# Softmax normalisation of the probability rows moved from VectorE to ScalarE in an attention and mixture-of-experts layer

## Chip, cores and metric

The kernel runs on all 8 cores of one Trainium2 chip, as one program on different data. The metric is device time in microseconds (us) of the slowest core. Two executions of the kernel before give 5368.27 and 5384.47 us, median 5376.37 us.

## The reference

Input `x` is (4, 2048, 2048) in float32. It is normalised per row (`_layernorm`, no affine part), and the layer returns `x + attention(xn) + moe(xn)`.

```python
q = heads(x @ Wq + bq); k = heads(x @ Wk + bk); v = heads(x @ Wv + bv)   # 16 heads of 128
scores = einsum('bhqd,bhkd->bhqk', q, k) / sqrt(2048)
scores = where(causal, scores, -inf)
attn = softmax(scores, axis=-1)
out = einsum('bhqk,bhkd->bhqd', attn, v) ... @ Wp + bp
# moe: 2 shared and 16 routed experts, 2048 -> 1408 -> 2048, relu;
# sigmoid router, the best 4 gates normalised; all experts are computed densely
```

## The kernel before

Each core takes half of one sequence: 1024 query rows of its own, 8 tiles of 128, against 2048 keys (its own 1024 and the sibling half's 1024, the latter masked by a bias `msk8`). The program has three stages.

- **p0** (lines 306 to 492): layer norm of the 16 row tiles, transposed by DMA into `xnf_own` and `xnf_sib`, and the router.
- **p1** (lines 522 to 889): attention, a loop over 16 heads `h`. Heads go in pairs: an even head first projects V for both (`wvb`, L810, 256 matmuls); an odd head ends with the output projection of both (L867, added into `acc` by VectorE at L884).
- **p2** (lines 898 to 1013): 18 experts, dense matmuls (L947, L954, L989).

Every engine has one queue in program order, written by the calls `T` (TensorE), `A` (ScalarE), `V` (VectorE), `DMA`; `wait=[...]` lists the tokens that an instruction waits for. An engine does nothing of what is queued behind a waiting instruction. The same Python order fills all queues.

For a query tile `tc` (0 to 7) of a head the pieces are:

- `plan_scores(tc)`: two matmuls of 512 keys of the sibling half (L664) into PSUM `psF[0]` and `psF[1]`, taken out by ScalarE (L674) into `scob`; then one or two matmuls for the own keys (L685) into the same two PSUM buffers, so that the first L685 waits until the first L674 has emptied `psF[0]`. The last own piece is taken out by VectorE (L695), another before it by ScalarE (L699). Then VectorE adds the diagonal mask (L705) and takes the row maximum (L711).
- `plan_scores_b(tc)`: ScalarE's exponential of the whole row, `L = (tc+9)*128` wide, float32 to bf16, with the row sum (L727); VectorE's reciprocal of the sum (L734) and the multiplication of the row by it (L737, bf16 in place in `prob`).
- `plan_transposes(tc)`: one DMA of SyncE's queue that transposes the row tile of `prob` into `atT` (L748). It waits for the normalised row and, since there is one `atT`, for the matmuls of the tile before that read it. `atT` lies on the same bytes as `wvb`.
- `plan_av(tc)`: `tc+9` matmuls of `atT` with V (L770) and ScalarE's evacuation into `outg` (L778).

`make_prep(h+1)` gives seven pieces for the next head: the weight DMAs, four K tiles (L564, 16 matmuls of 512 columns each, into `psF[4]` and `psF[5]`) and two Q tiles (L606, likewise). A head runs `plan_scores(0)`, `plan_scores(1)`, `plan_scores_b(0)`, `plan_scores(2)`, in even heads the V projection, and then for each `tc`:

```python
if tc + 1 < OWN: plan_scores_b(tc + 1)
if tc + 3 < OWN: plan_scores(tc + 3)
if nxt: nxt.pop(0)()          # one piece of the next head
plan_transposes(tc)
plan_av(tc)
```

So iteration 0 issues the weight DMAs, iterations 1 to 4 hold a K tile each, 5 and 6 a Q tile; iterations 0 to 4 hold scores of tile `tc+3`. Head 15 has no next head.

Of the kernel before, what the change touches and what calls it, by code (L numbers as in the profile page):

```python
# [11 lines left out]
AF = mybir.ActivationFunctionType  # L12
AX = mybir.AxisListType.X
ALU = AluOpType
# [136 lines left out]
def build_nc(dbg=False, phases=("p0", "p1", "p2")):  # L151
# [32 lines left out]
    def alloc(name, shape, dtype, off=None):  # L184
        if off is None:
            off = cur[0]
            per = int(np.prod(shape[1:])) * mybir.dt.size(dtype)
            cur[0] = (off + per + 31) & ~31
        return nc.alloc_sbuf_tensor_at(name, shape, dtype, offset=off)
# [19 lines left out]
    amx = alloc("amx", [128, 3, 8], F32)  # L209
# [26 lines left out]
    prob = alloc("prob", [128, 2, 2048], BF16, off=OVL + 60416)  # L236
# [15 lines left out]
    def B_(name):  # L252
        if name not in bufs:
            bufs[name] = Buf()
        return bufs[name]
# [4 lines left out]
    def V(fn, wait=()):  # L260
        return pl.on("vector", fn, wait, inc="ve")

    def A(fn, wait=()):
        return pl.on("scalar", fn, wait, inc="ac")
# [41 lines left out]
    if "p0" in phases:  # L306
        for ct in list(range(OWN, LCH)) + list(range(OWN)):
# [17 lines left out]
            for t_ in ts:  # L325
# [13 lines left out]
                                                 scale=-0.5), wait=[t1])  # L339
# [7 lines left out]
            if own:  # L347
# [11 lines left out]
                    scale=stab[:, ct, 0:1], bias=stab[:, ct, 1:2]),  # L359
# [6 lines left out]
                    scale=vt[:, sb, 2:3], bias=stab[:, ct, 1:2]),  # L366
# [22 lines left out]
            else:  # L389
# [7 lines left out]
                    scale=vt[:, sb, 2:3], bias=vt[:, sb, 3:4]),  # L397
# [124 lines left out]
    if "p1" in phases:  # L522
# [110 lines left out]
        for h in range(H):  # L633
# [84 lines left out]
            def plan_scores_b(tc, h=h):  # L718
                sl = tc % 3
                L = (tc + 9) * 128  # L720
                sc = B_("scob%d" % sl)
                am = B_("amx%d" % sl)
                pr = B_("prob%d" % (tc % 2))
                prold = pr.w()
                pr.wrd = {}
                pr.rdd = {}
                tex = A(lambda a, L=L, sl=sl, pp=tc % 2: a.activation(  # L727
                    prob[:, pp, 0:L], scob[:, sl, 0:L], AF.Exp, bias=amx[:, sl, 0:1],
                    scale=1.0, accum_out=amx[:, sl, 2:3]),
                    wait=[smx_tok[tc]] + prold)  # L730
                pr.did_w(tex)
                sc.did_r(tex)
                am.did_w(tex)
                trc = V(lambda v, sl=sl: v.reciprocal(amx[:, sl, 3:4], amx[:, sl, 2:3]),  # L734
                        wait=[tex])
                am.did_w(trc)
                tnm = V(lambda v, L=L, sl=sl, pp=tc % 2: v.tensor_scalar(  # L737
                    prob[:, pp, 0:L], prob[:, pp, 0:L], amx[:, sl, 3:4], None, ALU.mult),
                    wait=[trc, tex])
                pr.did_w(tnm)  # L740
                am.did_r(tnm)
                tnm_tok[tc] = tnm
# [46 lines left out]
            plan_scores(0)  # L789
            plan_scores(1)  # L790
            plan_scores_b(0)
            plan_scores(2)

# [38 lines left out]
            for tc in range(OWN):  # L832
                if tc + 1 < OWN:
                    plan_scores_b(tc + 1)
                if tc + 3 < OWN:
                    plan_scores(tc + 3)
                if nxt:
                    nxt.pop(0)()
                plan_transposes(tc)
                plan_av(tc)  # L840
# [252 lines left out]
```

How the kernel before makes its waits and increments, by code:

```python
            def _f(eng):  # L1027
                for ws, fn, inc, n in ops:
                    for s, v in ws:
                        eng.wait_ge(semh[s], v)
                    if fn is not None:
                        instr = fn(eng)
                        if inc is not None:
                            instr.then_inc(semh[inc], n)
```

## Time and profile before

| | |
|---|---|
| median of two executions | 5376.37 us |
| the profiled execution: device time | 4777.82 us |
| its span, slowest core (5) | 4776.3 us |
| spans of the 8 cores | 4756.1 to 4776.3 us |
| granted TensorE clock, mean of a core | 0.928 to 0.930 |
| stage p0, up to | 309 us |
| stage p1 | 309 to 1916 us, about 198.5 us for each pair of heads |
| stage p2 | 1916 us to the end |

The profile is of one execution, on core 5. Busy times of an engine are sums over its instructions. "Idle before, releaser" is time in which an engine did nothing before an instruction, and the instruction whose end it awaited. The chain of waits is followed back from the last instruction; a row of it is start, duration, and what was going on. "Clock" is the share of full speed granted to TensorE: 1.0 is 2.4 GHz, 0.5 is 1.2 GHz.

### The profile page before, as it was taken

What the parts mean: (1) busy time and instruction counts of PE and PEld (TensorE: products, weight loads), DVE (VectorE), ACT (ScalarE), POOL (GpSimd) and SP (SyncE); (2) the same over time, 40 slices, a digit from 0 to 9 for tenths busy, and PEclk for the clock granted to TensorE, in tenths of its full rate; (3) what the DMA queues carried; (4) which work ended last, traced back from release to release, by engine and by line L of the source; (5) the groups of instructions that cost most, each with busy time, mean ns of one, the idle gap of its engine ahead of it and who ended that gap; (6) DMA issues with size and microseconds to landing.
All of it is one profiled execution on the core that took longest, in us unless ns stands there. A gap on an engine that the chain in (4) does not pass through costs nothing.

```text
span 4776.3 us, 51141 instructions; the slowest of 8 cores (4756.1 to 4776.3 us)
## 1 busy us (share of the span) xinstructions
PE 3897.2 (82%) x19288; PEld 1852.9 (39%) x19288; DVE 1192.4 (25%) x1819; ACT 858.7 (18%) x1317; POOL 145.3 (3%) x256
## 2 busy tenths in 40 slices
PE   0036767667676675899999999999999999999997
PEld 0013424234243342344444444444444444444443
DVE  2223434434344344211112111221112111221112
ACT  2323232332323323001100011001100011001100
POOL 0000000000000000000000000000000000000000
PEclk9998878788787886699999999999999999999999
DMA  7332242322333223144434434344434434344434
GB/s 140 75 62 49 51 65 47 62 49 51 65 53 56 49 51 56 37 80 78 75 69 80 89 68 82 63 80 78 75 69 80 88 68 83 63 80 78 75 69 123
DMA packets 332254, 335.22 MB, mean 70 GB/s; under 512 B 300625, under 2 KB 301009, under 8 KB 307153
## 3 DMA queue, kind: packets, MB, share of 16 engines
q0 software_dynamic: 70848, 257.97, 29.6%
q1 hardware_dynamic: 260020, 65.60, 7.6%
q10 hardware_dynamic: 1152, 8.39, 0.4%
q8 instruction: 165, 2.70, 0.2%
q14 instruction: 69, 0.57, 0.0%
HBM read 499.69 MB, written 8.39 MB: 106 GB/s over the span
## 4 chain that ended last, share of the span: by engine, by line
PE 76%; DMA 10%; DVE 5%; issue 4%; ACT 4%; SPq 1%; DVEq 0%; ACTq 0%; POOLq 0%
PE psF L989 29%; PE psF L947 14%; PE psF L954 14%; PE psF L564 6%; DMA atT<-prob 6%; PE psF L810 5%; DVE acc L884 3%; PE psF L770 3%; ACT scob L674 2%; PE psF L908 1%; PE psF L867 1%; DMA atT<-wstream 1%; PE psF L606 1%; PE psF L685 1%; DMA lofm<-lobf 1%
## 5 line engine op out<-in xcount | busy, mean ns | idle before, releaser
L989 PE MATMUL psF<-w2b,hbuf 128*128 128x512 bf16 x6336 | 1370.4, 379 | 25.3 <-ACT hbuf L968 25.3
L947 PE MATMUL psF<-xnf_own,w1b 128*128 128x512 bf16 x3168 | 1201.8, 379 | 0.0
L954 PE MATMUL psF<-xnf_own,w1b 128*128 128x512 bf16 x3168 | 1201.7, 379 | 0.0
L989 PEld LDWEIGHTS psF<-w2b,hbuf 128*128 128x128 bf16 x6336 | 618.7, 98 | 777.0 <-issue 33.6
L1006 DVE SCALAR_TENSOR_TENSOR acc<-psF,gat,acc 128x512 f32<-128x512 f32 x512 | 384.2, 750 | 2071.9 <-PE psF L989 2071.9
L968 ACT ACTIVATE hbuf<-psF,b1t 128x512 bf16<-128x512 f32 x396 | 250.6, 684 | 2542.9 <-PE psF L947 2339.6
L947 PEld LDWEIGHTS psF<-xnf_own,w1b 128*128 128x128 bf16 x3168 | 310.2, 98 | 375.8 <-issue 2.8
L954 PEld LDWEIGHTS psF<-xnf_own,w1b 128*128 128x128 bf16 x3168 | 310.2, 98 | 374.3 <-issue 1.1
L770 PE MATMUL psF<-atT,vbuf 128*128 128x128 bf16 x1600 | 133.7, 245 | 179.8 <-DMA atT<-prob 177.9
L711 DVE TENSOR_REDUCE amx<-scob 128x1 f32<-128x1152 f32 (+7 forms) x128 | 232.9, 1819 | 13.3 <-DVE scob L705 0.2
L685 PE MATMUL psF<-kbuf,qbuf 128*128 128x512 bf16 (+1 forms) x192 | 73.5, 384 | 194.6 <-ACT scob L674 194.6
L884 DVE TENSOR_TENSOR acc<-acc,psF 128x512 f32<-128x512 f32 x256 | 175.9, 687 | 164.0 <-PE psF L867 137.3
L727 ACT ACTIVATE prob<-scob,amx 128x1152 bf16<-128x1152 f32 (+7 forms) x128 | 207.5, 1621 | 0.7 <-DVE amx L734 0.2
L674 ACT ACTIVATE scob<-psF,msk 128x512 f32<-128x512 f32 x256 | 161.3, 682 | 249.0 <-PE psF L664 247.3
L770 PEld LDWEIGHTS psF<-atT,vbuf 128*128 128x128 bf16 x1600 | 115.7, 110 | 217.5 <-issue 203.1
L431 PE MATMUL psF<-chl,xnf_own 128*128 128x16 bf16 x128 | 7.8, 174 | 226.2 <-DMA xnf_own<-xnbf 226.2
L867 PE MATMUL psF<-kbuf,outg 128*128 128x512 bf16 x256 | 94.9, 432 | 82.7 <-DMA atT<-wstream 47.4
L564 PE MATMUL psF<-xnf_own,wrA 128*128 128x512 bf16 x512 | 161.2, 486 | 0.0
L564 PE MATMUL psF<-xnf_sib,wrA 128*128 128x512 bf16 x512 | 144.7, 447 | 8.5 <-DMA wrA<-wstream 8.5
L664 PE MATMUL psF<-kbuf,qbuf 128*128 128x512 bf16 x256 | 102.2, 486 | 54.3 <-DVE scob L695 52.5
L685 PEld LDWEIGHTS psF<-kbuf,qbuf 128*128 128x128 bf16 x192 | 19.0, 99 | 294.1 <-issue 294.1
L810 PE MATMUL psF<-wvb,xnf_own 128*128 128x256 bf16 x1024 | 125.1, 289 | 0.3 <-DMA wvb<-wstream 0.2
(78 smaller groups left out, 1706.2 us busy)
## 6 DMA issues: line engine op xcount, KB each, us to landing
w2b<-wstream POOLq DMA_DIRECT2D x72, 1408.0 KB, 13.7
w1b<-wstream POOLq DMA_DIRECT2D x90, 1024.0 KB, 8.3
xstage<-xin POOLq DMA_DIRECT2D x16, 1024.0 KB, 7.0
w1b<-wstream POOLq DMA_DIRECT2D x18, 512.0 KB, 7.5
wrA<-wstream POOLq DMA_DIRECT2D x16, 512.0 KB, 6.5
wrB<-wstream POOLq DMA_DIRECT2D x16, 512.0 KB, 8.8
wvb<-wstream POOLq DMA_DIRECT2D x8, 1024.0 KB, 8.8
y<-acc ACTq DMA_DIRECT2D x8, 1024.0 KB, 11.8
```

Of the source, the lines that this page charges most:

```text
L564: mm = T(lambda t_, dc=dc, xt=xt, xo=xo, ps=ps: t_.matmul(ps[:], wrA[:, dc, :], xt[:, dc, xo:xo + 512], start=(dc == 0), stop=(dc == NCH - ...
L674: te = A(lambda a, j=j, sl=sl, ps=ps: a.activation(scob[:, sl, j * 512:(j + 1) * 512], ps[:], AF.Identity, scale=SCALE, bias=msk8[:, 0:1]) ...
L711: tmx = V(lambda v, L=L, sl=sl: v.reduce_max(amx[:, sl, 0:1], scob[:, sl, 0:L], axis=AX, negate=True), wait=sc.w() + amold)
L727: tex = A(lambda a, L=L, sl=sl, pp=tc % 2: a.activation(prob[:, pp, 0:L], scob[:, sl, 0:L], AF.Exp, bias=amx[:, sl, 0:1], scale=1.0, accum ...
L770: out_ps=out_ps, n=len(order): t_.matmul(out_ps[:, 0:128], vbuf[:, lci, hp * 128:(hp + 1) * 128], atT[:, slot, 0:128], start=(oi == 0), st ...
L810: mm = T(lambda t_, dc=dc, xt=xt, xo=xo, ps=ps: t_.matmul(ps[:, 0:256], xt[:, dc, xo:xo + 128], wvb[:, dc, :], start=(dc == 0), stop=(dc = ...
L884: tev = V(lambda v, tcq=tcq, dt=dt, ps=ps: v.tensor_tensor(acc[:, tcq, dt * 512:(dt + 1) * 512], acc[:, tcq, dt * 512:(dt + 1) * 512], ps[ ...
L947: mm0 = T(lambda t_, dc=dc, fci=fci, wslot=wslot, ps=ps0: t_.matmul(ps[:], w1b[:, wslot, dc, fci * 128:(fci + 1) * 128], xnf_own[:, dc, 0: ...
L954: mm1 = T(lambda t_, dc=dc, fci=fci, wslot=wslot, ps=ps1: t_.matmul(ps[:], w1b[:, wslot, dc, fci * 128:(fci + 1) * 128], xnf_own[:, dc, 51 ...
L968: te = A(lambda a, Fg=Fg, tt=tt, e=e, ps=ps: a.activation(hbuf[:, Fg, tt * 512:(tt + 1) * 512], ps[:], AF.Relu, bias=b1t[:, e, Fg:Fg + 1]) ...
L989: mm = T(lambda t_, fc=fc, tcq=tcq, wslot=wslot, ps=ps: t_.matmul(ps[:], hbuf[:, fc, tcq * 128:(tcq + 1) * 128], w2b[:, wslot, fc, :], sta ...
L1006: v.scalar_tensor_tensor(acc[:, tcq, dt * 512:(dt + 1) * 512], ps[:], gat[:, tcq, e - 2:e - 1], acc[:, tcq, dt * 512:(dt + 1) * 512], ALU. ...
```

## The change

The multiplication of the row by the reciprocal of its sum is issued on ScalarE as an activation `Identity` with the reciprocal as its per-partition scale, in place of VectorE's `tensor_scalar`. Its place in the Python order is the same, right behind the exponential and the reciprocal, so in ScalarE's queue it stands between the exponential of tile `tc+1` and the evacuations of the scores of tile `tc+3`. Its tokens are ScalarE's now; the transposing DMA and the next writers of `prob` wait for those.

```diff
                 trc = V(lambda v, sl=sl: v.reciprocal(amx[:, sl, 3:4], amx[:, sl, 2:3]),
                         wait=[tex])
                 am.did_w(trc)
-                tnm = V(lambda v, L=L, sl=sl, pp=tc % 2: v.tensor_scalar(
-                    prob[:, pp, 0:L], prob[:, pp, 0:L], amx[:, sl, 3:4], None, ALU.mult),
+                tnm = A(lambda a, L=L, sl=sl, pp=tc % 2: a.activation(
+                    prob[:, pp, 0:L], prob[:, pp, 0:L], AF.Identity,
+                    scale=amx[:, sl, 3:4]),
                     wait=[trc, tex])
                 pr.did_w(tnm)
                 am.did_r(tnm)
```

## Rows read from the trace of the kernel before

**Rows 1.** The page, busy time, share of the span and instructions of each engine.

```profile
PE 3897.2 (82%) x19288; PEld 1852.9 (39%) x19288; DVE 1192.4 (25%) x1819; ACT 858.7 (18%) x1317; POOL 145.3 (3%) x256
```

**Rows 2.** Windows: stretch, length, busy PE, PEld, DVE, ACT, POOL, clock, DMA.

```profile
748.00:947.00 199.00, 135.15 (x768) 71.94 (x768) 82.05 (x125) 64.13 (x105) 3.71 (x7) 0.83 0.32 55
1916.00:4776.00 2860.00, 2794.74 (x12736) 1259.79 (x12736) 450.23 (x608) 250.58 (x396) 106.82 (x180) 0.98 0.41 76
```

**Rows 3.** What L685 on TensorE waited for, all 192 (us, times).

```profile
  ACT scob L674: 194.6, 173
```

**Rows 4.** Timeline, iteration 2 of an even head: start, us, engine, line, operation.

```profile
793.63 1.27 ACT L674 ACTIVATE scob<-psF,msk 128x512 f32<-128x512 f32 x2
793.84 0.16 DVE L734 RECIPROCAL amx<-amx 128x1 f32<-128x1 f32 x1 [5.22 <-ACT prob L727]
794.11 0.62 DVE L737 TENSOR_SCALAR prob<-prob,amx 128x1536 bf16<-128x1536 bf16 x1
794.46 0.38 PE L685 MATMUL psF<-kbuf,qbuf 128*128 128x512 bf16 x1 [2.38 <-ACT scob L674]
```

**Rows 5.** Groups by shape: line, engine, shapes, count, busy us, mean ns, idle.

```profile
L727 ACT ACTIVATE prob<-scob,amx 128x2048 bf16<-128x2048 f32 x16 | 31.9, 1992 | 0.0
L727 ACT ACTIVATE prob<-scob,amx 128x1280 bf16<-128x1280 f32 x16 | 21.7, 1357 | 0.4 <-DVE amx L734 0.2
L727 ACT ACTIVATE prob<-scob,amx 128x1152 bf16<-128x1152 f32 x16 | 20.1, 1254 | 0.3
L395 ACT ACTIVATE xnbf<-xstage,vt 128x2048 bf16<-128x2048 f32 x8 | 16.7, 2093 | 6.0 <-DVE vt L391 3.5 <-DMA xnf_sib<-xnbf 2.5
L727 ACT ACT_TABLE_LOAD x1 | 1.3, 1283 | 0.1
L737 DVE TENSOR_SCALAR prob<-prob,amx 128x2048 bf16<-128x2048 bf16 x16 | 12.1, 753 | 1.7
```

**Rows 6.** Chain of waits, behind the V projection of an even head: start, us, what.

```profile
778.23 3.22 DMA atT<-prob
```

**Rows 7.** Timeline, iteration 6 of an even head.

```profile
830.73 0.75 DVE L737 TENSOR_SCALAR prob<-prob,amx 128x2048 bf16<-128x2048 bf16 x1
832.93 1.00 PE L770 MATMUL psF<-atT,vbuf 128*128 128x128 bf16 x15 [0.32 <-PE psF L606]
```

**Rows 8.** Timeline, start of an even head, ahead of its V projection.

```profile
747.24 1.27 ACT L674 ACTIVATE scob<-psF,msk 128x512 f32<-128x512 f32 x2
748.32 0.15 DVE L734 RECIPROCAL amx<-amx 128x1 f32<-128x1 f32 x1
```

**Rows 9.** Timeline of PE, ACT and DVE, start of an odd head.

```profile
849.94 0.48 PE L685 MATMUL psF<-kbuf,qbuf 128*128 128x384 bf16 x1 [0.50 <-ACT scob L674]
854.49 1.12 PE L770 MATMUL psF<-atT,vbuf 128*128 128x128 bf16 x9 [0.70 <-DMA atT<-prob]
...
852.37 1.27 ACT L674 ACTIVATE scob<-psF,msk 128x512 f32<-128x512 f32 x2 [0.49 <-PE psF L664]
...
850.88 0.55 DVE L695 TENSOR_SCALAR scob<-psF 128x384 f32<-128x384 f32 x1
853.47 0.15 DVE L734 RECIPROCAL amx<-amx 128x1 f32<-128x1 f32 x1
```

**Rows 10.** Timeline of PE in head 15, iterations 0, 2 and 4.

```profile
1838.00 1.12 PE L770 MATMUL psF<-atT,vbuf 128*128 128x128 bf16 x9 [1.51 <-DMA atT<-prob]
1848.41 1.33 PE L770 MATMUL psF<-atT,vbuf 128*128 128x128 bf16 x11 [0.79 <-DMA atT<-prob]
1860.03 1.55 PE L770 MATMUL psF<-atT,vbuf 128*128 128x128 bf16 x13 [0.81 <-DMA atT<-prob]
```

**Rows 11.** Chain of waits, K tiles of even and odd heads: start, us, what.

```profile
795.31 5.14 PE psF L564 x16
804.82 3.47 PE psF L564 x16
859.08 6.18 PE psF L564 x16
```

## Prediction

> **What bounds the kernel now.** I read the page first. ScalarE is busy for 858.7 us and VectorE for 1192.4 us of 4776.3 us [rows 1], so by busy time there seems to be room for an operation on either. That number decides nothing, so I went to the windows. The stage of the experts, from 1916 us on, keeps TensorE busy for 2794.7 of 2860 us [rows 2]; the change issues nothing there. A pair of heads takes about 199 us, and in it TensorE is busy for only 135 us, ScalarE for 64 and VectorE for 82 [rows 2]. No engine fills the stage: it is bound by a loop of waits, and the question is which engines' work lies in it.
>
> The third view answers that, what L685 waits for: 194.6 us in 173 waits, all for L674 [rows 3]. The chain of waits shows the loop in every iteration that has a K tile: L770 of one tile, L778, the exponential L727 of the next, the two L674, L685, the K tile's 16 matmuls L564, L770 again. The reason is the order of the queues. TensorE has put L664 into both PSUM buffers and can't issue L685, nor anything behind it (K tile, L770), before ScalarE has emptied the first; and ScalarE first has to do the exponential that stands ahead of L674 in its queue. The timeline shows what is not in the loop: VectorE's multiplication at 794.11 runs beside L674, which started at 793.63 [rows 4]. VectorE waited 5.22 us for the exponential before that. So VectorE has slack where ScalarE has none.
>
> **The change, part by part.**
>
> *Removed from VectorE*: 128 multiplications, 0.62 us at 1536 columns and 0.753 at 2048 [rows 4, 5], so by extrapolation 0.52 and 0.55 at the narrowest two, 1152 and 1280. They run beside ScalarE's evacuations, the cover that makes them nearly free. Only at a head's start do they stand ahead of VectorE's L695 of the next scores. I credit nothing for that, since ScalarE is later there after the change. The reciprocal stays.
>
> *Added to ScalarE*: 128 activations with a per-partition scale, in place in bf16. No row has this form. The nearest are the exponentials of the same widths with one per-partition operand: 1.254 us at 1152 columns, 1.357 at 1280, 1.992 at 2048 [rows 5], some 0.106 us for each 128 columns. An `Identity` to bf16 with two such operands took 2.093 at 2048 columns [rows 5]. So kind and function hardly matter, width does. The bounds are 0.753 us at 2048 columns, if ScalarE had VectorE's rate, and 2.093; I take the exponential's value, which is nearest in engine, operands and width.
>
> Here the skill speaks against the change: by the Trainium skill, ScalarE: Activation LUTs, Rules for kernel authors, a multiplication belongs on VectorE, which the page puts at up to about three times as fast for bf16 with one source. The rows say 1.992 against 0.753, or 2.6 times [rows 5]. By the page's three times the longest one would cost 2.26 us instead of 1.99, which is an estimate from the page and the row; the sum goes by the row.
>
> *The wait*: the new instruction waits on ScalarE for the reciprocal. Behind it in the queue stand the L674 of tile `tc+3`, for which L685 waits. In [rows 4] L674 starts at 793.63, the reciprocal at 793.84 with 0.16 us, and the multiplication that waits for it at 794.11. With the multiplication on ScalarE from 794.11 for 1.57 us (1536 columns, two steps above 1.357), and 0.09 us by which two ScalarE instructions overlap (two L674 of 0.68 us take 1.27), L674 starts at 795.59. That is its duration plus 0.39 us.
>
> *Iterations 1 to 4* of a head, each with the loop above: widths 1408, 1536, 1664 and 1792. By steps of 0.106 from 1.357 they take 1.46, 1.57, 1.68 and 1.78, in sum 6.49 us; with 4 x 0.39 that makes 8.05 us per head, all on the chain. Nothing takes it up again: the transposes are long landed when L770 starts.
>
> *Iterations 0 (even heads), 5, 6 and 7*: no cost. In iteration 0 of an even head the transpose behind the V projection takes 3.22 us [rows 6], and the scores of tile 3 would still end before it lands, about 0.4 us ahead by my count. In 5 and 6 there are no scores. The tightest is iteration 6: ScalarE's multiplication would run from 830.73 to 832.72, while the transpose that needs it waits for L770, which starts at 832.93 and ends at about 834 [rows 7]. What hides it is a Q tile and the single `atT`; without that cover it would cost some 1.2 us.
>
> *Start of an even head*: the reciprocal of tile 0 stands on VectorE behind the maximum of tile 1 and starts at 748.32, 1.08 us after the L674 of tile 2 [rows 8]. After the change L674 waits for it: 748.32 + 0.26 + 1.25 - 0.09 = 749.74, instead of 747.24. That is 2.50 us, which the L685 behind it passes on to the V projection.
>
> *Start of an odd head*: the same 2.50 us for tile 2. Then it cascades. L685 of tile 2 moves from 849.94 to 852.44 and its L695 to 852.96. From L695 to the next reciprocal VectorE has 2.59 us of work (850.88 to 853.47), so that comes at 855.55. The multiplication (1280 columns, 1.36) ends at 857.17 and L674 of tile 3 starts at 857.08 instead of 852.37: 4.7 us. L770 of tile 0 had waited 0.70 us for its transpose [rows 9], which takes up that much, and 4.0 us stay.
>
> *Head 15* has no K tiles and waits more for transposes. Its start costs 4.7 - 1.5 = 3.2 us, and iterations 1 to 4 cost 1.85, 1.96 - 0.79, 2.06 and 2.17 - 0.81 [rows 10], together 9.6 us.
>
> *TensorE's clock*: a K tile took 3.47 us where it was granted 1.0 all through, 5.14 where its first part ran at 0.5 (1.2 GHz) and 6.18 at an odd head's start, behind a stretch of sparse work [rows 11]. TensorE was idle for 2.38 us before L685 [rows 4], about as long in the other iterations, and behind most of these gaps the clock was at 0.5. On the chain an even head has one tile of 3.5 us and an odd head two. With 2 us more of idle time I expect that all of them begin at 1.2 GHz and cost at least 5.14: 8 x 1.67 + 7 x 2 x 1.67 = 37 us. The bounds are 0, and 92 us if every tile takes 6.18: 8 x (3 x 1.04 + 2.71) + 7 x (2 x 2.71 + 1.04). The Trainium skill has this direction too (TensorE: Matmul & The Clock Gate, Part 1: throttled is the default and activity releases it).
>
> *Sum*: 8 x (2.50 + 8.05) + 7 x (4.0 + 8.05) + 9.6 = 84.4 + 84.4 + 9.6 = 178 us, and with the clock 215 us. Against the profiled execution's own 4777.8 us that makes 4993 us. The two executions behind the median lie 599 us above it, and no view shows where; all added time is waiting in p1, so I carry the 215 us over unchanged: 5376 + 215 = 5591, or 4.0% more.
>
> **The rivals.**
>
> 1. *No clock term.* If the K tiles keep their mix of 3.5 and 5.1 us, the time is 5376 + 178 = 5554. For it: an idle stretch of 2.4 us already brings the fall in some iterations and not in others, so where the tiles fall may matter more than 2 us.
> 2. *A colder clock.* With every K tile at 6.18 us it is 5376 + 178 + 92 = 5646. For it: TensorE's idle time in a pair of heads would rise from 64 of 199 us to some 87 of 222. Against: once TensorE is busy, the clock has come back within the tile.
> 3. *A cheap multiplication.* Should ScalarE do it at VectorE's 0.5 to 0.7 us, an iteration costs 1.0 us rather than 2.0 and the total is near 90 us: 5466, within 2%. Against: no ScalarE row of that width is under 1.2 us.
> 4. *Off the chain* (the other side). If ScalarE's extra work ran under TensorE's, the removed VectorE work would be a small gain: 0.52 + 0.55 us ahead of L695 at each of 16 head starts, 17 us, so 5359, within 2%. This holds if L685 doesn't wait for L674; for it speaks ScalarE's 32% in the stage [rows 2], against it the 194.6 us [rows 3]. It decides only where L685 is ready at least 1.85 us after the first L674 has ended, and the wait says it is ready before.
> 5. *Freed weight loads.* The Trainium skill, SBUF — State Buffer, on who interferes with whom, has VectorE's fast modes lock GpSimd out while it writes descriptors for its DMAs. By rows: of the loads of GpSimd's queue only those of `wvb` and `wp` are on the chain, and 8 starts of 0.52 us would be 4 us of gain, too little to change the sign. It would make 5587 of my forecast.
> 6. *A table load with each `Identity`.* One load takes 1.28 us, and 256 would cost 328 us more. Against: there is one load at L727 in all [rows 5], though exponentials and `Identity` alternate throughout.
>
> **How the numbers follow.** My forecast, 178 us with a clock term of some 20 to 60 us, has a chance of 0.6 and gives 5574 to 5614. No clock term (or less than 178) has 0.18, the colder clock 0.12, the cheap multiplication 0.05, off the chain 0.03, freed loads 0.01 and table loads 0.01. The range 5515 to 5665 takes in the first three with the spread of the two executions shown (16 us) and an error of a fifth in the 178; it leaves out about 0.15. Two per cent, about what a measurement of this kernel tells from no change, is 107 us. Only rivals 3 and 4 end below that, so slower has 0.91, the same 0.08, and 0.01 is left for faster, of which I have no case.
>
> **What the changed profile would show.** The new ScalarE group should hold 128 instructions and about 207 us, with ScalarE near 1066 us and VectorE near 1111. L685's wait for L674 should rise from 194.6 us to about 400 (64 x 2 in the iterations, and the starts). The starts of an even head's V projection and of its first K tile should be 2.5 and 4.3 us later in the head; a pair of heads should take 22 to 27 us more, and p2 the same 2860 us. I am wrong if L674 starts right behind the exponential, if the new instructions are much shorter than 1.2 us, or if the K tiles' 3.47 us remain.

## The result and the profile after

The changed kernel is slower: the ratio to the kernel before is 1.0447, 95% interval 1.0403 to 1.0491. The median over all executions is 5163.38 us (13 of them, from 4992.57), and of the kernel before 4959.79 us (10, from 4770.66). In many executions of either kernel the cores of one die or both run at a lower granted clock (down to 0.79, where 0.93 before and 0.91 after are usual) and take longer; the ratio leaves those out, and the spans and stages below are of cores without it, on which the kernel before takes about 4775 us and the changed one 4993 to 5006.

The profiled executions have spans of 4776.3 us before (core 5) and 5004.0 us after (core 6), 227.7 us more. The added time is all in the stage of attention. From the first K tile's matmul to the first matmul behind the stage the 8 cores take 1612.3 us before and 1838.0 us after in the median, 225.7 us more; what follows takes 2843 to 2847 us in both.

The page of the changed kernel, busy time of each engine ([rows 1]). ScalarE has 202 us more, VectorE 80 us less. 335 of TensorE's 19288 matmul records are missing on this core, among them 127 in each of two lines of the experts' stage and 10 of the K tiles.

```profile
PE 3921.8 (78%) x18953; PEld 1868.4 (37%) x19288; DVE 1112.0 (22%) x1691; ACT 1060.7 (21%) x1445; POOL 145.9 (3%) x256
```

Windows of the changed kernel, a pair of heads and the stage of the experts, columns as in [rows 2]. The pair takes 228.7 us instead of 199, and TensorE is busy for only 5 us more in it; a window of the same length in the experts' stage looks as before.

```profile
761.20:989.90 228.70, 140.01 (x758) 73.76 (x768) 72.04 (x108) 89.42 (x120) 3.72 (x7) 0.79 0.27 48
2142.40:5002.40 2860.00, 2781.45 (x12482) 1260.27 (x12736) 450.23 (x608) 250.70 (x396) 107.32 (x180) 0.98 0.42 76
```

What L685 waited for in the changed kernel ([rows 3]: 194.6 us), on the profiled core 6, where 185 of 192 matmuls have a record. Core 1 has a record of each: 389.2 us after and 193.1 before. So the few waits of core 6 that are put down to "remote" seem to belong to the same stall.

```profile
  ACT scob L674: 365.4, 133
  remote: 29.4, 6
```

The new ScalarE groups by shape, narrowest and widest (columns as in [rows 5]). They are as long as the exponentials of the same width. The idle time ahead of them is the wait for the reciprocal: 20.4 us over 16 instructions for tile 0 and 19.5 for tile 1, some 1.2 us each, and 0.4 us each for the later tiles.

```profile
L737 ACT ACTIVATE prob<-prob,amx 128x2048 bf16<-128x2048 bf16 x16 | 32.0, 2002 | 6.9 <-DVE amx L734 6.9
L737 ACT ACTIVATE prob<-prob,amx 128x1152 bf16<-128x1152 bf16 x16 | 20.1, 1255 | 20.4 <-DVE amx L734 20.4
```

The timeline of the changed kernel in iteration 3 of an even head, ScalarE and then TensorE (in [rows 4] the same place in iteration 2). L674 starts 2.19 us after the accumulator's read-out, where it had started beside it, and L685 sits behind it for 4.51 us instead of 2.4.

```profile
860.94 0.19 ACT L727 ACTIVATION_READ_ACCUMULATOR prob<-scob,amx 128x1 f32 x1
861.54 1.68 ACT L737 ACTIVATE prob<-prob,amx 128x1664 bf16<-128x1664 bf16 x1 [0.41 <-DVE amx L734]
863.13 1.25 ACT L674 ACTIVATE scob<-psF,msk 128x512 f32<-128x512 f32 x2
...
863.94 1.06 PE L685 MATMUL psF<-kbuf,qbuf 128*128 128x512 bf16 x2 [4.51 <-ACT scob L674]
864.80 6.17 PE L564 MATMUL psF<-xnf_sib,wrA 128*128 128x512 bf16 x16
```

The K tiles as a group (columns as in [rows 5], TensorE), both on core 5, which has every record: first the changed kernel, 343.2 us over 1024 matmuls or 335 ns each, then the kernel before, 305.9 us or 299 ns each. (The mean in the rows counts each matmul from its own start, and neighbours overlap.)

```profile
L564 PE MATMUL psF<-xnf_sib,wrA 128*128 128x512 bf16 x512 | 173.8, 514 | 7.0 <-DMA wrA<-wstream 7.0
L564 PE MATMUL psF<-xnf_own,wrA 128*128 128x512 bf16 x512 | 169.4, 504 | 0.0
...
L564 PE MATMUL psF<-xnf_own,wrA 128*128 128x512 bf16 x512 | 161.2, 486 | 0.0
L564 PE MATMUL psF<-xnf_sib,wrA 128*128 128x512 bf16 x512 | 144.7, 447 | 8.5 <-DMA wrA<-wstream 8.5
```

### The profile page after: what moved, and what is told of

The parts are those of the page before. It is cut to its first block, busy times and chain, and to the rows that moved or that the text cites. A ratio compares the mean times of both kernels' runs of the same rounds, so it can differ in the third digit from the quotient of the medians.

```text
span 5004.0 us, 50680 instructions; the slowest of 8 cores (4976.8 to 5004.0 us)
## 1 busy us (share of the span) xinstructions
PE 3921.8 (78%) x18953; PEld 1868.4 (37%) x19288; DVE 1112.0 (22%) x1691; ACT 1060.7 (21%) x1445; POOL 145.9 (3%) x256
## 4 chain that ended last, share of the span: by engine, by line
PE 72%; DMA 8%; issue 6%; DVE 6%; ACT 5%; another core or an unknown queue 1%; SPq 1%; DVEq 0%; ACTq 0%; POOLq 0%
PE psF L990 27%; PE psF L955 14%; PE psF L948 13%; PE psF L564 7%; PE psF L811 5%; DMA atT<-prob 5%; DVE acc L885 3%; PE psF L771 2%; ACT scob L674 2%; ACT prob L727 2%; PE psF L685 2%; PE psF L909 1%; DMA xstage<-xin 1%; PE psF L868 1%; DMA atT<-wstream 1%
## 5 line engine op out<-in xcount | busy, mean ns | idle before, releaser
L955 PE MATMUL psF<-xnf_own,w1b 128*128 128x512 bf16 x3168 | 1202.0, 379 | 7.0 <-issue 0.3
L948 PE MATMUL psF<-xnf_own,w1b 128*128 128x512 bf16 x3041 | 1153.8, 379 | 0.0
L685 PE MATMUL psF<-kbuf,qbuf 128*128 128x512 bf16 (+3 forms) x185 | 82.3, 446 | 394.8 <-ACT scob L674 365.4
L771 PE MATMUL psF<-atT,vbuf 128*128 128x128 bf16 x1600 | 135.7, 247 | 161.4 <-DMA atT<-prob 161.0
L737 ACT ACTIVATE prob<-prob,amx 128x1152 bf16<-128x1152 bf16 (+7 forms) x128 | 208.4, 1628 | 79.9 <-DVE amx L734 79.9
L674 ACT ACTIVATE scob<-psF,msk 128x512 f32<-128x512 f32 x256 | 160.2, 675 | 240.7 <-PE psF L664 232.5
L727 ACT ACTIVATE prob<-scob,amx 128x1152 bf16<-128x1152 f32 (+7 forms) x128 | 207.4, 1620 | 0.8
L685 PEld LDWEIGHTS psF<-kbuf,qbuf 128*128 128x128 bf16 x192 | 19.6, 102 | 492.8 <-issue 492.8
L771 PEld LDWEIGHTS psF<-atT,vbuf 128*128 128x128 bf16 x1600 | 118.5, 112 | 195.9 <-issue 180.8
L431 PE MATMUL psF<-chl,xnf_own 128*128 128x16 bf16 x128 | 7.8, 174 | 225.7 <-DMA xnf_own<-xnbf 225.7
L564 PE MATMUL psF<-xnf_sib,wrA 128*128 128x512 bf16 x511 | 173.9, 515 | 9.9 <-DMA wrA<-wstream 9.9
L695 DVE TENSOR_SCALAR scob<-psF 128x128 f32<-128x128 f32 (+3 forms) x128 | 62.8, 491 | 442.8 <-PE psF L685 442.6
## 6 DMA issues: line engine op xcount, KB each, us to landing
wvb<-wstream POOLq DMA_DIRECT2D x8, 1024.0 KB, 10.1
```

Of the source, the lines that this page charges most:

```text
L564: mm = T(lambda t_, dc=dc, xt=xt, xo=xo, ps=ps: t_.matmul(ps[:], wrA[:, dc, :], xt[:, dc, xo:xo + 512], start=(dc == 0), stop=(dc == NCH - ...
L674: te = A(lambda a, j=j, sl=sl, ps=ps: a.activation(scob[:, sl, j * 512:(j + 1) * 512], ps[:], AF.Identity, scale=SCALE, bias=msk8[:, 0:1]) ...
L727: tex = A(lambda a, L=L, sl=sl, pp=tc % 2: a.activation(prob[:, pp, 0:L], scob[:, sl, 0:L], AF.Exp, bias=amx[:, sl, 0:1], scale=1.0, accum ...
L771: out_ps=out_ps, n=len(order): t_.matmul(out_ps[:, 0:128], vbuf[:, lci, hp * 128:(hp + 1) * 128], atT[:, slot, 0:128], start=(oi == 0), st ...
L948: mm0 = T(lambda t_, dc=dc, fci=fci, wslot=wslot, ps=ps0: t_.matmul(ps[:], w1b[:, wslot, dc, fci * 128:(fci + 1) * 128], xnf_own[:, dc, 0: ...
L955: mm1 = T(lambda t_, dc=dc, fci=fci, wslot=wslot, ps=ps1: t_.matmul(ps[:], w1b[:, wslot, dc, fci * 128:(fci + 1) * 128], xnf_own[:, dc, 51 ...
```

## The experiments

The theory is the prediction's, call it *place*: what stands in ScalarE's queue ahead of L674 holds up L685 and all of TensorE's work behind it, by the wait plus the length, and the longer idle stretch lets the clock fall. The rivals are *load* (ScalarE simply has more to do, or the row is finished later for its transpose), *wait alone*, *length alone*, and *no clock effect*. "Stage" is the length of the attention stage as measured above, the median of the cores (1612.3 us before, 1838.0 after). Times of K tiles are of a core that has every record.

**The same work, behind the evacuations.** The multiplication stays on ScalarE, but is issued after `plan_scores`.

```diff
 if tc + 1 < OWN: plan_scores_b(tc + 1)     # now without tnm
 if tc + 3 < OWN: plan_scores(tc + 3)
+if tc + 1 < OWN: plan_norm(tc + 1)         # tnm: ScalarE's Identity
```

(and `plan_norm(0)` behind `plan_scores(2)`)

> ScalarE does the same 128 multiplications, but each stands in its queue behind the score evacuations (L674, L699) of the same iteration instead of ahead of them. Queue-place theory (L685 waits for L674, so only what stands ahead of L674 costs): nearly all of the loss is gone, span 4776 to 4795 us, ratio to before 1.000 to 1.004, L685's wait for L674 back near 195 us. Rival, load or late rows (ScalarE's extra 208 us, or the later finished probability row that the transpose needs, is what costs): the row is finished later still, so the span stays at 5000 us or more, ratio 1.045 or more.

Measured: span 4779.4 us, stage 1617.5 us, so 5 of the 225.7 us are left, and L685's wait for the evacuation is back at 200.3 us. The timeline of this kernel, ScalarE in one iteration (L728 is the exponential, L675 and L700 the evacuations, L745 the multiplication): 

```profile
787.62 1.57 ACT L728 ACTIVATE prob<-scob,amx 128x1536 bf16<-128x1536 f32 x1
789.08 0.20 ACT L728 ACTIVATION_READ_ACCUMULATOR prob<-scob,amx 128x1 f32 x1
789.18 1.26 ACT L675 ACTIVATE scob<-psF,msk 128x512 f32<-128x512 f32 x2
790.48 0.60 ACT L700 ACTIVATE scob<-psF 128x512 f32<-128x512 f32 x1
790.97 1.57 ACT L745 ACTIVATE prob<-prob,amx 128x1536 bf16<-128x1536 bf16 x1
795.02 0.37 ACT L787 ACTIVATE outg<-psF,bvt 128x128 bf16<-128x128 f32 x1 [2.48 <-PE psF L779]
```

The multiplication lies in time in which ScalarE waited anyway, for the K tile to pass on TensorE. Load falls for this order of the queue: the same 128 instructions cost 5 us here and 226 us one call earlier, though the row is finished later here (3.5 us from the read-out's start to the multiplication's end, against 2.3 us in the changed kernel).

**Half the length.** VectorE multiplies the left half of the columns, ScalarE the right half (in tiles with an odd number of blocks 128 columns more), at the place of the change.

```diff
+tnv = V(... v.tensor_scalar(prob[:, pp, 0:Lh], prob[:, pp, 0:Lh], amx[:, sl, 3:4], None, ALU.mult) ...)
-tnm = A(... prob[:, pp, 0:L] ...)
+tnm = A(... prob[:, pp, Lh:L] ...)
```

> VectorE multiplies the first half of the columns and ScalarE the second half, both at the place of the change. Queue-place theory with cost = fixed hop + duration: each step before L674 is shorter by some 0.65 us than in the changed kernel, 5 to 6 such steps a head, so 16 x 3.4 = 54 us less than the changed kernel: span about 4950 us, ratio 1.036. Rival, the wait for the reciprocal is the main cost and the multiplication's length minor: less than 20 us off, ratio 1.042 or more.

Measured: span 4929.8 us, stage 1769.6 us, 68 us less than the changed kernel's where 54 had been expected. The expectation left the clock out: the K tiles take 17 us less than in the changed kernel (326.6 us against 343.2).

**The wait without the length.**

```diff
 tnm = V(... v.tensor_scalar(prob[:, pp, 0:L], ...))      # as before
+twt = A(lambda a, sl=sl: a.activation(amx[:, sl, 4:5], amx[:, sl, 2:3], AF.Identity,
+        scale=amx[:, sl, 3:4]), wait=[trc, tex])
```

> VectorE does the whole multiplication as before; ScalarE has one extra activation of 128x1 (into an unused column of amx) that waits for the reciprocal, at the place of the change. Queue-place theory: what stays is the hop and a 0.2 us instruction, about 0.5 us in each of iterations 1 to 4 and 1.5 us and more at the starts, where the reciprocal stands behind a maximum on VectorE: 16 x 4 = 64 us, span about 4840 us, ratio 1.013. Rival, the multiplication's length is all that counts: ratio within 0.003 of 1.

Measured: span 4872.0 us, stage 1713.7 us, 101 us more than before, where 64 had been expected. The timeline of ScalarE in this kernel:

```profile
807.90 0.19 ACT L727 ACTIVATION_READ_ACCUMULATOR prob<-scob,amx 128x1 f32 x1
808.51 0.29 ACT L740 ACTIVATE amx<-amx 128x1 f32<-128x1 f32 x1 [0.41 <-DVE amx L734]
808.71 1.25 ACT L674 ACTIVATE scob<-psF,msk 128x512 f32<-128x512 f32 x2
```

L674 starts 0.81 us after the read-out instead of 0.09, so 0.72 us later, not 0.5: the one-column activation takes 0.29 us, and I had set 0.2. The expectation also left the clock out; the K tiles take 328.2 us here, 22 us more than before.

**The length without the wait.** ScalarE copies the row in place, as wide as the multiplication, right behind the exponential; VectorE multiplies after it.

```diff
+tcp = A(lambda a, L=L, pp=tc % 2: a.activation(prob[:, pp, 0:L], prob[:, pp, 0:L], AF.Copy), wait=[tex])
 tnm = V(... v.tensor_scalar(prob[:, pp, 0:L], ...), wait=[trc, tcp])
```

> The kernel before (reciprocal and multiplication on VectorE) with an in-place copy of the row by ScalarE right behind the exponential, as wide as the multiplication of the change but not waiting for the reciprocal; VectorE's multiplication waits for the copy. It holds the length without the wait. Queue-place theory with two parts, wait and length: the stage grew by 226 us after the change and by 101 us with the wait and a 0.29 us instruction alone, so the length should be worth 226 - 101 + the 0.29 us of each instruction, 140 to 165 us: span 4915 to 4945 us, ratio 1.03 to 1.035. Rival, the wait is free once the length is there (both the same stall): span about 4985 to 5004 us. Rival, the wait is the whole: below 4820 us.

Measured on cores 0 to 3: spans of 4916.3 to 4928.7 us and a stage of 1770.2 us, 158 us more than before. So wait and length both cost: 101 us and 158 us when each is alone, 225.7 together. That is 33 us less than the sum of the two. Two things count twice in that sum: the wait's own 0.29 us instruction, about 5 to 6 times a head (some 25 us), and part of the clock, since the K tiles grow by about 22 and 29 us in the two kernels and by 37 in the change. This is arithmetic; no run separates the two.

**Twice the length.** A second pass over the same row, a copy in place.

```diff
 tnm = A(... AF.Identity, scale=amx[:, sl, 3:4]), wait=[trc, tex])
+tnm = A(lambda a, L=L, pp=tc % 2: a.activation(prob[:, pp, 0:L], prob[:, pp, 0:L], AF.Copy), wait=[tnm])
```

> The changed kernel with a second pass of ScalarE over the same row (a copy in place, same width) right behind the multiplication. Queue-place theory: each step ahead of L674 grows by about another 1.5 us, and iteration 0 of even heads and iteration 6 lose their cover (0.5 to 1.2 us each): some 9 us a head, 148 us more than the changed kernel, span about 5150 us, ratio 1.078. Rival, only the first wait counts (the second pass is hidden): the same as the changed kernel, 1.045.

Measured: span 5175.9 us, stage 2013.0 us, 175 us more than the changed kernel's; the expectation of 148 was low, and the rival of a hidden second pass is out. From half to full to double length the stage goes 1769.6, 1838.0, 2013.0 for a mean of 0.99, 1.63 and 3.16 us of ScalarE's passes over a row. The K tiles have 17 and 11 us of these two differences; the rest is 80 and 107 us for each microsecond, 5 and 6.7 steps a head. The prediction counts five in an even head and six in an odd one (four iterations, and one or two multiplications at the head's start). That the second pass has more fits its loss of cover in iterations 0 and 6, which was expected; no run shows that part alone.

**Keeping TensorE busy in the gap.** 12 extra matmuls of 512 columns behind L664 of tiles 3 to 7, their result read by nobody.

```diff
+if tc >= 3:
+    for i in range(12):
+        tf = T(... t_.matmul(psF[3][:], qbuf[:, ksl, tc*128:(tc+1)*128],
+                             kbuf[:, ksl, 1024:1536], start=True, stop=True) ...)
 atiles = [(a0, min(a0 + 512, LA)) for a0 in range(0, LA, 512)]
```

> The changed kernel with 12 extra matmuls of 512 columns (operands of L664, into psF[3], which nobody reads in this stage) between L664 and L685 of tiles 3 to 7, where TensorE was idle for 2.4 to 4.7 us. They take 2.6 us at 2.4 GHz and 5.1 us at 1.2 GHz. Theory, part of the loss is the clock that falls in the longer idle stretch (L564 took 339 ns a matmul after the change, 299 before, 1024 of them: 41 us): L564 falls to 220 to 250 ns, some 100 us are gained, span about 4900 us, ratio 1.026. Rival, the K tiles' length has another cause than the idle stretch (operands, contention): L564 stays at 339 ns and the span at 5004 us or above, ratio 1.045 or more.

Measured: span 4905.2 us, ratio 1.0284 (1.0264 to 1.0305), stage 1745.9 us: 92 us shorter with 960 matmuls more. The K tiles of this kernel, on core 5:

```profile
L564 PE MATMUL psF<-xnf_sib,wrA 128*128 128x512 bf16 x512 | 133.2, 420 | 6.9 <-DMA wrA<-wstream 6.9
L564 PE MATMUL psF<-xnf_own,wrA 128*128 128x512 bf16 x512 | 121.9, 394 | 0.0
```

They take 249 ns a matmul (255.1 us) instead of 335, 88 us over the 1024, which is nearly the whole gain. (The 339 ns of the expectation are of core 6, ten of whose records are missing.) So the longer K tiles were the clock's doing, and idleness in the gap is what brought it down. ([rows 11] shows a tile of 3.47, one of 5.14 and one of 6.18 us; on core 5, of the 60 K tiles that are computed inside a head's loop, 45 take about 3.6 us from the first matmul's start to the last one's end here, and none in the changed kernel.)

**The same in the kernel before**, with 6 extra matmuls.

> The kernel before with 6 such extra matmuls at the same place (1.3 us at 2.4 GHz, 2.6 us at 1.2 GHz, in an idle stretch of 2.4 us). Clock theory: L564 falls from 299 ns to about 240, some 50 us are gained, span about 4725 us, ratio 0.99. Rival: no gain, ratio 1.00 or above.

Measured on cores 0 to 3: spans of 4697.0 to 4706.2 us and a stage of 1550.8 us, 62 us shorter than before, with the K tiles at 228 ns a matmul (233.8 us). The kernel before paid for the clock too.

**Evacuations ahead of the exponential.** The kernel before, with two calls of the loop swapped.

```diff
-if tc + 1 < OWN: plan_scores_b(tc + 1)
 if tc + 3 < OWN: plan_scores(tc + 3)
+if tc + 1 < OWN: plan_scores_b(tc + 1)
```

> The kernel before (multiplication on VectorE) with the scores of tile tc+3 put ahead of the exponential of tile tc+1 in each iteration, so that ScalarE evacuates L664 before it does the exponential. Queue-place theory: the exponential too leaves the loop, 6.5 us and more a head in iterations 1 to 4, and TensorE's idle stretch before L685 shrinks under 1 us, which keeps the clock up in the K tiles: 110 + 60 us, span about 4610 us, ratio 0.965. Rival, the transposes or VectorE's maximum become late and take the gain back: ratio 0.99 to 1.01.

Measured: ratio 0.9733 (0.9711 to 0.9755), span 4645.4 us, stage 1489.1 us. The chain of waits of this kernel shows two K tiles at full clock in a row, 6 us apart, where before the K tiles of a head had started 7.8 to 10.3 us apart:

```profile
747.83 3.45 PE psF L564 x16
751.28 0.63 PE psF L770 x11
752.85 0.69 ACT scob L674
754.00 3.47 PE psF L564 x16
```

123 us are gained and not 170, 43 of them in the K tiles (262.7 us): the first K tile of a head keeps its 4.6 to 5.6 us, and in iteration 5 the chain now goes through VectorE's maximum, the reciprocal and the multiplication before the transpose.

**The same order with the multiplication on ScalarE.**

> The same order with the multiplication on ScalarE as in the change. Queue-place theory: nothing of it stands ahead of L674 in iterations 1 to 4; the row is finished some 1 us after the matmuls of the tile before, so each transpose starts up to 1 us later: span 4640 to 4690 us, ratio 0.975, far below the changed kernel's 1.045 with the same work on ScalarE. Rival, ScalarE's load: as far above the run evac_first as the change lies above before, that is by 4.5% and more.

Measured: ratio 0.9952 (0.9935 to 0.9969), span 4753.5 us, stage 1586.7 us. That is 98 us over the run before it, less than half of the 226 us that the same edit costs in the old order and more than the 0 to 50 us expected. What L685 waited for here, and in the run with the multiplication on VectorE:

```profile
  ACT scob L674: 201.1, 170
```

```profile
  ACT scob L674: 95.0, 173
```

The difference of 106 us is the same stall. I had counted iterations 1 to 4 as cleared, and they are not. By tile, on core 1 and as a mean of the heads, L685 of tile 2 waits 2.4 us longer than in the run before it: at a head's start `plan_scores_b(0)` still stands ahead of `plan_scores(2)`. L685 of tile 4 waits 1.6 us longer in even and 3.1 us longer in odd heads: the multiplication of tile 1 in iteration 0 stands ahead of `outg` and of tile 4's L674. And L685 of tiles 6 and 7 wait 0.5 and 1.4 us longer, behind the multiplications of tiles 3 and 4 of the iteration before. The timeline shows the last of these, ScalarE and then TensorE:

```profile
792.88 1.68 ACT L737 ACTIVATE prob<-prob,amx 128x1664 bf16<-128x1664 bf16 x1 [1.71 <-DVE amx L734]
...
795.29 1.26 ACT L674 ACTIVATE scob<-psF,msk 128x512 f32<-128x512 f32 x2
...
796.12 0.38 PE L685 MATMUL psF<-kbuf,qbuf 128*128 128x512 bf16 x1 [2.22 <-ACT scob L674]
```

The multiplication waits 1.71 us here for a reciprocal that now stands behind VectorE's maximum, and with K tiles of 3.6 us ScalarE isn't through with it when the next scores are ready. So the cause is again what stands ahead of L674, but with the faster loop the length of ScalarE's whole queue begins to count, which *place* alone doesn't say. By these waits the two last tiles have some 31 of the 106 us; no run separates them.

**VectorE's multiplication ahead of its maximum**, on top of the swapped order.

```diff
 if tc + 3 < OWN: plan_scores(tc + 3)       # without L705 and L711
 if tc + 1 < OWN: plan_scores_b(tc + 1)
+if tc + 3 < OWN: plan_max(tc + 3)          # L705, L711
```

(and at the head's start `plan_max(1)` behind `plan_scores_b(0)`)

> The run evac_first with, in addition, VectorE's reciprocal and multiplication of tile tc+1 put ahead of its mask and maximum (L705, L711) of tile tc+3, at the head's start too. In evac_first the chain went through L711 of tile 7, the reciprocal and the multiplication before the transpose of iteration 5, and through L711 of tile 1 at an odd head's start. If that is so, 1 to 2 us a head are gained: span about 4620 us, ratio 0.967. Rival, the maximum, now later, delays the exponential by as much: 4645 us or more, ratio 0.973.

Measured: span 4641.0 us, stage 1480.8 us: 8 us shorter than the run with the swapped order, against 16 to 32 expected, and by the span 4 us, 0.1%, which is no more than executions of the kernel before differ by. It lies 2.8% below the kernel before by the spans.

**Six extra matmuls ahead of the first transpose**, on top of that.

> The run norm_before_max with 6 extra matmuls of 512 columns (into psF[3], read by nobody) behind the scores of tile 3, where TensorE waits for the first transpose. If the first K tile's 4.6 to 5.6 us (3.45 for the others) comes from the clock that fell there, it is shorter by 1 to 2 us in 15 heads: 20 us less than norm_before_max. Rival: the extra matmuls only delay the first L770 (2.6 us at 1.2 GHz): no gain or up to 16 us more.

Measured on cores 4 to 7: spans of 4621.8 to 4634.2 us, against 4623.2 to 4635.1 us of the same cores without the extra matmuls; stage 1477.9 us against 1479.4, so 1.5 us less where 20 had been expected. The chain of waits of the two kernels, first K tile of an even head, without and with them:

```profile
738.00 5.40 PE psF L564 x16
```

```profile
741.55 3.52 PE psF L564 x16
```

The clock was the cause of the first tile's length, as expected: all K tiles together take 234.3 us here and 258.8 without the extra matmuls (core 5). But nothing of it is left at the end. By the same core's trace, mean of seven pairs, the gain of an even head (the second L770 is 1.5 us earlier) lasts to its last L770, 1.2 us earlier; then the first L770 of the odd head comes 1.4 us later than without them, which is 2.5 us lost at that head's start, and the pair takes 180.7 us against 180.8. So these matmuls cost more at an odd head's start than they save in its first K tile (1.9 us). The remaining 0.3 us at its last L770 mostly go before the next head; no run shows to what.

## Why the prediction was right, and where it was wrong

The direction, the mechanism and the size came out; the predicted time, 5591 us, and its range did not hold the median of 5163 us. **The step that failed is the last of the sum**: "The two executions behind the median lie 599 us above it, and no view shows where; ... so I carry the 215 us over unchanged". I took 5376 us as the level of the kernel. It was the median of two executions at the upper end; eight more, from 4771 to 5363 us, brought it to 4960 us. The profiled execution, 4777.8 us, was evidence against 5376 that I had in hand: the two figures of one kernel lay 599 us apart, and the range should have reached down to the lower. By the profiled execution's own time the sum gave 4993 us; it measured 5005.5 us, and its share, 215 of 4778 us or 4.5%, stands beside the ratio of 1.0447 (4.8% by the two profiled spans). Dividing by 5376, I had written 4.0%.

That the two medians differ by 203.6 us, near the 215 of the sum, is in part luck. Of the 13 executions of the changed kernel six take 4993 to 5006 us and seven 5163 to 5620; the median is the lowest of these seven, and one more execution would move it by 70 to 80 us either way.

Step by step:

- *What bounds the kernel.* Right. Moving the same instructions behind the evacuations took back 220 of 225.7 us.
- *Length of the new instructions.* Right: 1255 to 2002 ns, against 1254 to 1992 taken from the exponentials; ScalarE 1060.7 us busy (1066 forecast), VectorE 1112.0 (1111).
- *The step, duration plus 0.39 us.* It measured 2.19 us from the read-out for 1664 columns, against 0.09 before, so 2.10 us: 1.68 + 0.42.
- *Start of an even head, 2.50 us.* From the L674 of tile 1 to that of tile 2 it is 5.11 us after and 2.57 us before (747.24 in [rows 8], that of tile 1 at 744.67): 2.54 us. *Start of an odd head, 4.7 and 4.0 us*: the L674 of tile 3 comes 4.4 us later after that of tile 0, and the first L770 3.5 us.
- *The clock, 37 us.* It measured 37 us (343.2 against 305.9 us on core 5; 33 to 41 us on the six cores with every record), and the extra matmuls showed the cause. Without it 188 us remain, where 178 were summed. The total came out as forecast, its parts less so: an even head's four tiles grew by 2.4 us (1.67 forecast) and an odd head's by 2.5 (3.34), since some tiles of 3.5 us went to 6 and not to 5.14.
- *No cost in p2, no table loads, transposes still hidden.* Right: 2843 to 2847 us behind the attention stage in both; one table load at L727 as before; L771's wait for its transposes fell from 177.9 to 161.0 us.
- *L685's wait, about 400 us.* 389.2 us on core 1.
- *A pair of heads, 22 to 27 us more.* 28.4 us on core 5 in the mean of seven pairs, and its trace shows where: 2.4 us at an even head's start (2.5 forecast), 3.9 at an odd head's (4.0), and from L770 of tile 0 to that of tile 4 10.9 us in an even head (8.05 + 1.67 forecast) and 11.0 in an odd one (8.05 + 3.34); the rest of a head adds less than 0.5 us. So the term that was too small is that of the even head's iterations, by 1.2 us a pair, two thirds of it the clock. The 30 us between the two windows above are of two different cores and one pair, in which one transpose took 8.8 us beside 7.6.

Of the rivals, *off the chain* and *a cheap multiplication* fell by the result; *no clock term* and *a colder clock* by the K tiles' 335 ns (an average of 5.4 us a tile, between 5.14 and 6.18). *A table load with each `Identity`* fell by the single load at L727. *Freed weight loads*, by the Trainium skill, SBUF — State Buffer, Who interferes with whom, left no sign of a gain: the loads on the chain took a median of 8.8 us to land before and 10.1 after (`wvb`), 5.4 and 5.1 (`kbuf`), 5.1 and 5.1 (`atT`). No run tests that rule by itself.

## What to carry to other kernels

Ask of an instruction to be added not how busy its engine is but what stands behind it in that engine's queue and who waits for that: here 202 us of work on an engine that was 18% busy cost 226 us, or 5 us when issued one call later. In this kernel an evacuation that frees a PSUM buffer for a waiting TensorE belonged ahead of everything that can wait, the exponential too (2.7% gained). And where two figures for the same kernel lie far apart, a forecast should be made as a share of each, with a range that holds both.

## What was not expected of the hardware

- Work thrown away paid: 960 matmuls with an unread result, 232 us of TensorE's busy time over the 952 recorded, shortened the stage by 92 us, because the granted clock stayed up (mean of a core 0.942 to 0.944 with them, 0.908 to 0.912 without). The Trainium skill, TensorE: Matmul & The Clock Gate, Part 1, says that activity releases the throttle; the trace agrees.
- A ScalarE activation of one column takes 0.29 us, and a dependent one waits 0.41 us from the exponential's read-out through VectorE's reciprocal. A tiny instruction that waits for another engine cost 101 us when put 128 times at this place.
